# Dilated attention: the biased copy of the input row is made after the split of the projected keys instead of before it

## The chip, the cores and the metric

The kernel runs on one core of one Trainium2 chip. The metric is device time in microseconds (us) for one execution of the whole program; lower is better. The engines named below are TensorE (PE, with its weight loads PEld), VectorE (DVE), ScalarE (ACT), GpSimd (POOL) and SyncE (SP), whose queue issues the transfers between memory and the on-chip buffers.

## The reference, cut to what matters

The program computes six sublayers over x of 16 x 512 x 256, in float32. Only the second one is touched:

```python
x = x + 0.5 * _L0_ffn_ref(_layernorm(x), ...)       # stage f1
x = x + _L0_attn_ref(_layernorm(x), ...)            # stage a1, the changed one
x = x + 0.5 * _L0_ffn_ref(_layernorm(x), ...)       # stage f2
x = x + 0.5 * _L1_ffn_ref(_layernorm(x), ...)       # c1
x = x + _L1_attn_ref(_layernorm(x), ...)            # b1
x = x + 0.5 * _L1_ffn_ref(_layernorm(x), ...)       # c2

# _L0_attn_ref: (branch, offset) pairs (0, 0), (1, 0), (1, 1) with dilations 1, 2, 2
for br, off in pairs:
    xs = x[:, off::r, :].reshape(b_, -1, 128, 256)   # segments of 128 tokens
    att = _mha(xs, Wqkv[br], bqkv[br], Wout[br], bout[br])   # 16 heads of 16
    full = zeros_like(x).at[:, off::r, :].set(att)
res = sum of the three, each times 1/3
```

## The kernel before, in words

The stages run one after another, the attention stage from about 1103 to 2200 us. It handles the 16 batch rows of 512 tokens in turn. A row is eight units of work: four segments of 128 tokens for branch 0 (units u = 0 to 3) and four for branch 1 (u = 4 to 7). A unit t is one segment: PE multiplies queries and keys of 16 heads (`scores`, L1366), DVE takes the maxima (`maximum`, L1566), ACT the exponentials in four groups of heads, here called quads 0 to 3 (`exps`, L1512), PE turns them (`turn_ex`, L1377), DVE copies them (`turned`, L1572), PE multiplies by the values, DVE divides (L1595), and PE and DVE make one eighth of the output of the row before (`put_out`, L1417 and L1604).

Every engine has its own instruction stream, written out by hand in a function `step(t)`; the order within it is the order of execution, and engines meet only at semaphores. Work for later units is done ahead. In unit t, PE projects keys or queries of unit t + 5 (AHEAD is 5), ACT adds the bias and writes the full value and its rounded high part (`project`, L1498; the mark is `a_qk`), and POOL makes the low part: `split_qk(t + AHEAD)`. For queries that is one instruction (L1285). For keys it is five: the difference (L1291), and two copies each of the high and low part, multiplied with the parity of the head (L1296).

POOL has two more jobs in a row r. In unit u = 2 it computes the root and the normalised input of row r + 2 (L135, L137, `scale` L1275), and in unit u = 7 it adds the output bias to the input of row r + 1 (`biased`, L1266: four instructions that read `xt` and write `xb`, mark `g_xb`). Before it does that, `biased(r + 1)` waits until DVE has made the last eighth of the output of row r - 1 (`d_y`), because that output still reads the `xb` buffer of the same parity. POOL reads `xb` for nothing else; DVE uses it one row later.

There are two `xt` buffers. SP's `step(r)` waits for `d_h(r)`, the normalised input made two rows earlier, and for `g_xb(r)`, then issues `load(r + 2)` (L1227, 512 KB), then waits for `d_y(r - 1)` and stores a row (L1243). So the load of row r + 3 waits for `biased(r + 1)`, which is issued in unit u = 7 of row r. DVE needs the loaded row in unit u = 1 of the following row: `half_statistics` (L1632) waits for the load, takes the statistics of two of its four tiles, and takes the other two later in the same unit; the means (L1640) follow in unit u = 2. DVE's order in a unit u = 1 is: divide and turn the next input, maxima of quads 0 and 1, the output part, the reciprocal, the copy of quad 3 of the unit before, the first half of the statistics, the maximum of quad 2, the turned reciprocal, the maximum of quad 3, the copy of quad 0, the second half of the statistics, the copies of quads 1 and 2. PE's `scores(t)` waits for ACT's quad 3 of unit t - 1 and for DVE's copy of quad 2 of unit t - 1, since all share banks of PSUM.

Of the kernel before, what the change touches and what calls it, by code (L numbers as in the profile page):

```python
# [67 lines left out]
def turns(engine, count, unroll, step):  # L68

    groups = count // unroll  # L70
    assert groups * unroll == count and groups >= 2
    for u in range(unroll):
        step(Turn(0, u, unroll))
    if groups > 2:
        with engine.Fori(1, groups - 1) as g:
            for u in range(unroll):
                step(Turn(g, u, unroll))
    for u in range(unroll):
        step(Turn(groups - 1, u, unroll))
# [74 lines left out]
def slot_wait(e, tracks, t):  # L154

    k = len(tracks)
    e.wait_ge(tracks[t.step % k].sem, t.group * (16 * (t.unroll // k)) + 16 * (t.step // k + 1))
# [966 lines left out]
def dilated_attention(nc, name, src, dst, w):  # L1124

    with ExitStack() as ctx:
# [4 lines left out]
        AHEAD = SEGS + 1  # L1131
# [40 lines left out]
        rows, units = B, B * UR  # L1172
# [50 lines left out]
        with nc.Block() as block:  # L1223
            @block.sync
            def _(sp):
                def load(r):
                    sp.dma_start(xt[r.step % 2][:], row_tiles(src, r)).then_inc(s_ld[r.step % 2].sem, 16)  # L1227

                load(first_row)
                sp.dma_start(ident[:], w["ident"]).then_inc(s_id, 16)  # L1230
                for n, (k, t) in enumerate(split):
                    sp.dma_start(raw[n], w[k].rearrange("r (c p) d -> p r c d", p=P)).then_inc(s_raw[n], 16)
                for t, k in ((bq, "abq"), (bk, "abk"), (bv, "abv"), (par, "parity")):
                    sp.dma_start(t[:], w[k]).then_inc(s_p, 16)
                load(first_row + 1)
                sp.dma_start(spread[0:SLOT], w["spread"]).then_inc(s_w, 16)
                sp.dma_start(bo[:].rearrange("p r d -> p (r d)"),
                             w["abo"].rearrange("(o r) d -> o (r d)", o=1).to_broadcast([P, BR * D])).then_inc(s_w, 16)
                sp.dma_start(wo[:], w["ao"].rearrange("r (c p) d -> p r c d", p=P)).then_inc(s_w, 16)

                def store(r):
                    d_y.wait(sp, r)
                    sp.dma_start(row_tiles(dst, r), yt[r.step % 2][:]).then_inc(s_st[r.step % 2].sem, 16)  # L1243

                def step(r):
                    if (r + 2).exists(last=rows):
                        norm.d_h.wait(sp, r)
                        g_xb.wait(sp, r)
                        load(r + 2)
                    if (r - 1).exists():  # L1250
                        store(r - 1)
                turns(sp, rows, ROWS, step)
                store(last_row)
                for k in range(2):
                    sp.wait_ge(s_st[k].sem, 16 * (rows // 2))

            @block.gpsimd
            def _(pool):
                pool.wait_ge(s_c, 1)

                def biased(r):
                    slot_wait(pool, s_ld, r)
                    if (r - 2).exists():
                        d_y.wait(pool, r - 2)
                    for v in range(SEGS):
                        last = pool.tensor_tensor(xb[r.step % 2][:, v, :], xt[r.step % 2][:, v, :], bos[:, 2, :], ALU.add)  # L1266
                    g_xb.mark(last)

                def scale(r):
                    k = r.step % 2  # L1270
                    norm.g_ln.wait(pool, r, "rstd", alone=True)
                    if (r - 1).exists():
                        t_hT.wait(pool, r - 1, "7", alone=True)
                    for v in range(SEGS):
                        last = pool.tensor_scalar(h[:, v, :], xt[k][:, v, :], norm.mv[:, k, v, 0:1],  # L1275
                                                  norm.rstd[:, k, v:v + 1], ALU.subtract, ALU.mult)
                    norm.d_h.mark(last)

                def split_qk(t):
                    br, j = ur_of(t) // SEGS, t.step % SEGS  # L1280
                    c, x = j % DC, full[t.step % 2]
                    a_qk.wait(pool, t)
                    if j >= DC:
                        hi, lo = (a[:, c, :] for a in qT[br])
                        g_qk.mark(pool.tensor_tensor(lo, x[:], hi.bitcast(F32), ALU.subtract))  # L1285
                        return
                    hi = k_hi[t.step % 2]
                    k_mark = Turn(t.group, t.step // SEGS * DC + j, ROWS * UR // 2)
                    if (t - 1).exists():
                        g_qk.wait(pool, t - 1)  # L1290
                    g_kl.mark(pool.tensor_tensor(k_lo[:], x[:], hi[:].bitcast(F32), ALU.subtract))  # L1291
                    for n, part in enumerate((hi, k_lo)):
                        if n:
                            g_kl.wait(pool, k_mark)
                        for e in range(2):
                            last = pool.tensor_tensor(kz[br][n][:, c, e, :], part[:].bitcast(F32),  # L1296
                                                      par[:, e:e + 1].to_broadcast([P, S]), ALU.mult)
                    g_qk.mark(last)

                norm.root(pool, first_row)  # L1300
                norm.root(pool, first_row + 1)
                scale(first_row + 1)
                pool.wait_ge(s_p, 16 * 4)
                for j in range(AHEAD):
                    split_qk(first_unit + j)
                pool.wait_ge(s_b, 4)
                biased(first_row)

                def step(t):
                    u, r = ur_of(t), row_of(t)  # L1310
                    if u == 2 and (r + 2).exists(last=rows):
                        norm.root(pool, r + 2)
                        scale(r + 2)
                    if u == 7 and (r + 1).exists(last=rows):
                        biased(r + 1)
                    if (t + AHEAD).exists(last=units):
                        split_qk(t + AHEAD)
                turns(pool, units, ROWS * UR, step)

            @block.tensor  # L1320
# [1000 lines left out]
```

## Time and profile before

| what | value |
| --- | --- |
| time, median of 3 runs | 4007.72 us (4007.39 to 4008.62) |
| the profiled execution: its time, its span | 4008.62 us, 4006.8 us |
| granted TensorE clock, mean | 0.983 |
| busy over the whole span | PE 95%, PEld 83%, DVE 80%, ACT 77%, POOL 67% |
| mean DMA rate | 35 GB/s |

The profile is one execution. Its span is the time from the first to the last recorded instruction, and 1.8 us of its time lie outside of it. The busy share of PE is modelled and says little by itself: in a stage where engines hand work to one another in a circle, each can look nearly full, while the time is set by the circle. The rows further down are taken from the attention stage.

### The profile page before, as it was taken

What the parts mean: (1) busy time and instruction counts of PE and PEld (TensorE: products, weight loads), DVE (VectorE), ACT (ScalarE), POOL (GpSimd) and SP (SyncE); (2) the same over time, 40 slices, a digit from 0 to 9 for tenths busy, and PEclk for the clock granted to TensorE, in tenths of its full rate; (3) what the DMA queues carried; (4) which work ended last, traced back from release to release, by engine and by line L of the source; (5) the groups of instructions that cost most, each with busy time, mean ns of one, the idle gap of its engine ahead of it and who ended that gap; (6) DMA issues with size and microseconds to landing.
All of it is one profiled execution on the core that took longest, in us unless ns stands there. A gap on an engine that the chain in (4) does not pass through costs nothing. (4 is left out here: it accounts for less than half of the span.)

```text
span 4006.8 us, 81018 instructions
## 1 busy us (share of the span) xinstructions
PE 3796.5 (95%) x28440; PEld 3314.4 (83%) x28440; DVE 3198.6 (80%) x7738; ACT 3098.6 (77%) x7882; POOL 2701.5 (67%) x2202
## 2 busy tenths in 40 slices
PE   7999999999979999999998799999999997999989
PEld 6888888888858888888886688888888887898878
DVE  7888888888758888888875788888888877756667
ACT  6888888888759999999996688888888877632166
POOL 7888888888655554655541788888888866512266
PEclk9999999999989999999999899999999998999999
DMA  2000000000010000000000100000000003331342
GB/s 66 17 17 17 17 17 17 17 17 17 9 44 18 13 23 14 22 23 13 23 7 18 64 17 17 17 17 17 17 17 17 17 12 98 122 105 53 127 151 90
DMA packets 135061, 141.90 MB, mean 35 GB/s; under 512 B 8672, under 2 KB 131968, under 8 KB 134656
## 3 DMA queue, kind: packets, MB, share of 16 engines
q1 hardware_dynamic: 134656, 136.71, 10.7%
q8 instruction: 228, 3.74, 0.4%
q14 instruction: 177, 1.45, 0.1%
HBM read 80.06 MB, written 56.62 MB: 34 GB/s over the span
## 5 line engine op out<-in xcount | busy, mean ns | idle before, releaser
L300 POOL TENSOR_TENSOR f_grid<-f_sim 128x1024 f32<-128x1024 f32 x512 | 969.4, 1910 | 0.1
L1512 ACT ACTIVATE a_ex<-a_p_s,a_mneg 128x128 f32<-128x128 f32 x2048 | 728.2, 409 | 89.9 <-DVE a_mneg L1566 89.9
L686 DVE SCALAR_TENSOR_TENSOR f_p_u<-f_grid,f_te,f_p_dot 128x1024 f32<-128x1024 f32 x512 | 653.2, 1276 | 111.7 <-PE f_p_dot L106 65.3
L308 POOL TENSOR_TENSOR f_q<-f_q 128x1024 f32<-128x1024 f32 x256 | 607.9, 2386 | 123.1 <-ACT f_q L558 121.0
L695 DVE SCALAR_TENSOR_TENSOR f_q<-f_p_u,f_rz,f_grid 128x1024 f32<-128x1024 f32 x512 | 650.9, 1271 | 0.4
L539 ACT ACTIVATE f_grid<-f_grid,f_negm 128x1024 f32<-128x1024 f32 x512 | 559.2, 1142 | 0.0
L1512 ACT ACTIVATION_READ_ACCUMULATOR a_ex<-a_p_s,a_mneg 128x1 f32 x2048 | 508.8, 248 | 0.0
L443 PE MATMUL f_p_y<-f_eup,f_wT 128*128 128x256 f32 x2048 | 472.9, 379 | 0.0
L438 PE MATMUL f_p_y<-f_wdn,f_hs 128*128 128x256 f32 x2048 | 468.4, 382 | 0.0
L443 PEld LDWEIGHTS f_p_y<-f_eup,f_wT 128*128 128x128 f32 x2048 | 388.5, 190 | 57.7
L438 PEld LDWEIGHTS f_p_y<-f_wdn,f_hs 128*128 128x128 f32 x2048 | 378.8, 190 | 49.7
L1566 DVE TENSOR_REDUCE a_mneg<-a_p_s 128x4 f32<-128x512 f32 x512 | 335.0, 675 | 6.7 <-PE a_p_s L1366 6.7
L1572 DVE COPY a_exT<-a_p_s 128x512 f32<-128x512 f32 x384 | 254.4, 684 | 91.9 <-PE a_p_s L1377 91.6
L425 PE MATMUL f_p_wT<-f_ident,f_q 128*128 128x128 f32 x2048 | 269.1, 274 | 22.1 <-POOL f_q L308 20.8
L425 PEld LDWEIGHTS f_p_wT<-f_ident,f_q 128*128 128x128 f32 x2048 | 229.2, 140 | 44.3 <-POOL f_q L308 34.5
L552 ACT ACTIVATE f_hs<-f_p_hid 128x512 f32<-128x512 f32 x256 | 152.1, 594 | 141.4 <-PE f_p_hid L106 140.7
L1377 PE MATMUL a_p_s<-a_ident,a_ex 128*128 128x128 f32 x1536 | 241.6, 283 | 10.6 <-ACT a_ex L1512 10.4
L558 ACT ACTIVATE f_q<-f_q 128x2048 f32<-128x2048 f32 x128 | 244.4, 1909 | 0.0
L287 POOL TENSOR_TENSOR f_cand<-f_tx,f_ty 128x512 f32<-128x512 f32 x128 | 136.9, 1070 | 147.4 <-DVE f_ty L650 147.1
L1377 PEld LDWEIGHTS a_p_s<-a_ident,a_ex 128*128 128x128 f32 x1536 | 166.7, 141 | 53.1 <-ACT a_ex L1512 37.6
L546 ACT COPY f_wT<-f_p_wT 128x512 f32<-128x512 f32 x256 | 148.2, 579 | 76.6 <-PE f_p_wT L425 76.6
L523 ACT COPY f_sim<-f_p_sim 128x512 f32<-128x512 f32 x128 | 74.1, 579 | 142.2 <-PE f_p_sim L106 142.2
(646 smaller groups left out, 11029.3 us busy)
## 6 DMA issues: line engine op xcount, KB each, us to landing
x_f<-f_yt SPq DMA_DIRECT2D x64, 256.0 KB, 2.1
f_xt<-x SPq DMA_DIRECT2D x32, 256.0 KB, 2.9
a_xt<-x_f SPq DMA_DIRECT2D x16, 512.0 KB, 3.8
x_a<-a_yt SPq DMA_DIRECT2D x16, 512.0 KB, 2.9
f_xt<-x_a SPq DMA_DIRECT2D x32, 256.0 KB, 2.9
c_xt<-x_f SPq DMA_DIRECT2D x16, 512.0 KB, 4.7
x_c<-c_yt SPq DMA_DIRECT2D x16, 512.0 KB, 3.1
b1p_xt<-x_c SPq DMA_DIRECT2D x16, 512.0 KB, 3.9
```

The costliest lines, as they stand in the source:

```text
L300: g_grid.mark(pool.tensor_tensor(grid[v][:, hd, :].rearrange("p (i j) -> p i j", i=XROWS), sx[:, hd, :].unsqueeze(2).to_broadcast([P, XROW ...
L308: g_pair.mark(pool.tensor_tensor(q[v][:, 2 * k, :], q[v][:, 2 * k, :], q[v][:, 2 * k + 1, :], ALU.add), f"{v}{k}")
L425: last = pe.matmul(p_wT[:, e, :], q[v][:, hd, (k * HALF + e) * P:(k * HALF + e + 1) * P], ident[:], is_transpose=True, start=hd == 0, stop ...
L438: pe.matmul(p_y[:, v, :], hs[t.step % 2][:, e, v * P:(v + 1) * P], wdn[:, e, :], start=e == 0, stop=False)
L443: last = pe.matmul(p_y[:, v, :], wT[v][:, e, :], eup[:, e, :], start=False, stop=e == EC - 1)
L539: a_exp.mark(act.activation(grid[v][:, hd, :], grid[v][:, hd, :], ACT.Exp, bias=negm[:, v, hd:hd + 1]), f"{v}{hd}")
L686: d_mask.mark(dve.scalar_tensor_tensor(out=p_u[:], in0=grid[v][:, hd, :], scalar=te[:, v, hd, TOP - 1:TOP], in1=p_dot[:], op0=ALU.is_ge, o ...
L695: d_mul.mark(dve.scalar_tensor_tensor(out=q[v][:, hd, :], in0=p_u[:], scalar=rz[:, v, hd:hd + 1], in1=grid[v][:, hd, :], op0=ALU.mult, op1 ...
L1377: last = pe.transpose(p_e[i][:, n, :], ex[t.step % 2][:, i, n, :], ident[:])
L1512: last = act.activation(ex[t.step % 2][:, i, n, :], p_s[i][:, n, :], ACT.Exp, bias=mneg[:, i, n:n + 1], accum_out=z[t.step % 2][:, i, n:n ...
L1566: d_max.mark(dve.tensor_reduce(mneg[:, i, :], p_s[i][:], AX.X, ALU.max, negate=True), str(i))
L1572: d_ex.mark(dve.tensor_copy(exT[t.step % 2][:, i, :, :], p_e[i][:]), str(i))
```

## The change

In POOL's `step(t)` the two last statements change places. In unit u = 7 of each row POOL now does the split of unit t + 5 first, and the biased copy of row r + 1 after it. In the other seven units nothing changes. The other engines' streams and SP's are the same.

```diff
                     if u == 2 and (r + 2).exists(last=rows):
                         norm.root(pool, r + 2)
                         scale(r + 2)
+                    if (t + AHEAD).exists(last=units):
+                        split_qk(t + AHEAD)
                     if u == 7 and (r + 1).exists(last=rows):
                         biased(r + 1)
-                    if (t + AHEAD).exists(last=units):
-                        split_qk(t + AHEAD)
                 turns(pool, units, ROWS * UR, step)
```

In unit u = 7 the split is that of unit t + 5, which is u = 4 of the next row, the first keys of branch 1, so five instructions. POOL's stream around it before, from the last query split of unit 6 to the first instruction of the next unit (`waits` names the semaphores that an instruction waits for; `a_kz1h` and `a_kz1l` are the parity copies of branch 1, `a_k0h` and `a_k1h` the high parts of two successive units):

```order
L1285 TENSOR_TENSOR a_qT0l<-a_full,a_qT0h 128x512 [waits a1_a_qk] x2
L1266 TENSOR_TENSOR a_xb<-a_xt,a_bos 128x256 [waits a1_d_y,a1_s_ld0]
L1266 TENSOR_TENSOR a_xb<-a_xt,a_bos 128x256 x3
L1291 TENSOR_TENSOR a_kl<-a_full,a_k0h 128x512 [waits a1_g_qk,a1_a_qk]
L1296 TENSOR_TENSOR a_kz1h<-a_k0h,a_par 128x512 x2
L1296 TENSOR_TENSOR a_kz1l<-a_kl,a_par 128x512 [waits a1_g_kl]
L1296 TENSOR_TENSOR a_kz1l<-a_kl,a_par 128x512
L1291 TENSOR_TENSOR a_kl<-a_full,a_k1h 128x512 [waits a1_g_qk,a1_a_qk]
```

And the same place of POOL's stream in the changed kernel:

```order
L1285 TENSOR_TENSOR a_qT0l<-a_full,a_qT0h 128x512 [waits a1_a_qk] x2
L1291 TENSOR_TENSOR a_kl<-a_full,a_k0h 128x512 [waits a1_g_qk,a1_a_qk]
L1296 TENSOR_TENSOR a_kz1h<-a_k0h,a_par 128x512 x2
L1296 TENSOR_TENSOR a_kz1l<-a_kl,a_par 128x512 [waits a1_g_kl]
L1296 TENSOR_TENSOR a_kz1l<-a_kl,a_par 128x512
L1266 TENSOR_TENSOR a_xb<-a_xt,a_bos 128x256 [waits a1_d_y,a1_s_ld0]
L1266 TENSOR_TENSOR a_xb<-a_xt,a_bos 128x256 x3
L1291 TENSOR_TENSOR a_kl<-a_full,a_k1h 128x512 [waits a1_g_qk,a1_a_qk]
```

The four instructions of L1266 have moved behind the five of one key split, with their waits for the output and the load; this happens once in each of 15 rows, and no instruction is added or removed.

## Rows read from the trace of the kernel before

**Rows 1.** Stretch, us, busy PE PEld DVE ACT POOL, granted clock, DMA: units u=1, 2:

```profile
1606.90:1614.92 8.02, 8.02 (x99) 6.77 (x98) 7.60 (x18) 7.41 (x38) 7.88 (x8) 1.00 0.09 31
1614.92:1622.94 8.02, 8.02 (x99) 6.77 (x98) 6.67 (x18) 7.40 (x38) 3.24 (x5) 1.00 0.01 2
```

**Rows 2.** Timeline (start us, us, engine, line), first scores of two units:

```profile
1606.92 0.39 PE L1366 MATMUL a_p_s<-a_kz0l,a_qT0h 32*128 32x256 f32 x4
...
1614.94 0.39 PE L1366 MATMUL a_p_s<-a_kz0l,a_qT0h 32*128 32x256 f32 x4
```

**Rows 3.** Timeline, ACT, from unit u = 7 to u = 1:

```profile
1599.27 0.81 ACT L1498 ACTIVATE a_k0h<-a_p_pr,a_bk 128x512 fp32r<-128x512 f32 x1
...
1606.36 0.31 ACT L1512 ACTIVATION_READ_ACCUMULATOR a_ex<-a_p_s,a_mneg 128x1 f32 x1
...
1608.72 0.37 ACT L1512 ACTIVATE a_ex<-a_p_s,a_mneg 128x128 f32<-128x128 f32 x1 [0.61 <-DVE a_mneg L1566]
...
1611.73 0.42 ACT L1512 ACTIVATE a_ex<-a_p_s,a_mneg 128x128 f32<-128x128 f32 x1
```

**Rows 4.** Timeline, SP queue, same stretch:

```profile
1601.42 0.36 SPq L1243 DMA_DIRECT2D x_a<-a_yt  x1
1604.40 0.36 SPq L1227 DMA_DIRECT2D a_xt<-x_f  x1
```

**Rows 5.** Timeline, POOL, same stretch:

```profile
1601.53 2.79 POOL L1266 TENSOR_TENSOR a_xb<-a_xt,a_bos 128x256 f32<-128x256 f32 x4 [8.11 <-DVE a_yt L1604]
1604.28 1.27 POOL L1291 TENSOR_TENSOR a_kl<-a_full,a_k0h 128x512 fp32r<-128x512 f32 x1
...
1607.51 2.03 POOL L1296 TENSOR_TENSOR a_kz1l<-a_kl,a_par 128x512 fp32r<-128x512 f32 x2
```

**Rows 6.** All issues of L1227, the loads of a_xt:

```profile
L1227 SPq DMA_DIRECT2D a_xt<-x_f x16: 359/360/525, 1106.2 to 1989.6; - x16
...
DMA to landing us min/median/max: 3.7/3.8/6.2
```

**Rows 7.** Timeline, DVE, unit u = 1 and start of u = 2:

```profile
1610.04 0.73 DVE L1632 BATCH_NORM_STATS2 a_bs<-a_xt 128x6 f32<-128x256 f32 x2
1610.69 0.67 DVE L1566 TENSOR_REDUCE a_mneg<-a_p_s 128x4 f32<-128x512 f32 x1
...
1613.43 1.31 DVE L1572 COPY a_exT<-a_p_s 128x512 f32<-128x512 f32 x2
...
1615.97 1.28 DVE L1566 TENSOR_REDUCE a_mneg<-a_p_s 128x4 f32<-128x512 f32 x2
```

**Rows 8.** Timeline, POOL, start of the stage and end of row 0:

```profile
1145.19 1.27 POOL L1291 TENSOR_TENSOR a_kl<-a_full,a_k0h 128x512 fp32r<-128x512 f32 x1 [3.01 <-ACT a_k0h L1498]
...
1150.47 2.77 POOL L1266 TENSOR_TENSOR a_xb<-a_xt,a_bos 128x256 f32<-128x256 f32 x4
...
1183.07 1.29 POOL L1291 TENSOR_TENSOR a_kl<-a_full,a_k0h 128x512 fp32r<-128x512 f32 x1 [3.78 <-ACT a_k0h L1498]
...
1191.06 1.28 POOL L1291 TENSOR_TENSOR a_kl<-a_full,a_k1h 128x512 fp32r<-128x512 f32 x1 [2.70 <-ACT a_k1h L1498]
...
1214.99 1.29 POOL L1291 TENSOR_TENSOR a_kl<-a_full,a_k0h 128x512 fp32r<-128x512 f32 x1 [3.93 <-ACT a_k0h L1498]
```

**Rows 9.** Timeline, SP queue, start of the stage, two issues merged:

```profile
1153.32 58.18 SPq L1227 DMA_DIRECT2D a_xt<-x_f  x2
```

**Rows 10.** Timeline, DVE, statistics of row 3:

```profile
1224.84 0.73 DVE L1632 BATCH_NORM_STATS2 a_bs<-a_xt 128x6 f32<-128x256 f32 x2
```

**Rows 11.** Source L1296, who waited for it (us, times):

```profile
  ACT a_full L1498: 9.3, 2
```

**Rows 12.** Busy time and granted clock, start of the stage, 2 us each:

```profile
1151.00:1153.00 2.00, 1.11 (x8) 0.64 (x7) 0.80 (x2) 2.00 (x14) 2.00 (x4) 1.00 0.00 0
1153.00:1155.00 2.00, 1.12 (x5) 0.93 (x5) 0.59 (x1) 2.00 (x14) 0.24 (x1) 0.65 0.15 27
1155.00:1157.00 2.00, 1.34 (x21) 1.16 (x24) 1.18 (x3) 1.38 (x4) 0.54 (x1) 0.50 0.74 244
```

## The prediction

> **What bounds the kernel now.** I read the busy table first, but it does not decide. In the attention stage a unit takes 8.02 us: PE's first scores of two successive units start at 1606.92 and 1614.94 [rows 2]. PE is shown busy for all 8.02 us of both units, ACT for 7.4, DVE for 7.60 in the unit with the statistics (u = 1) and 6.67 in the next [rows 1]. PE is not what sets the 8.02. In row 0 PE has no output part to make, and POOL's splits still follow one another after 7.99 us, 1183.07 to 1191.06 [rows 8].
>
> So I looked for a circle in the timelines. ACT's last exponential of a unit ends at 1606.36 + 0.31 = 1606.67; PE starts the next scores at 1606.92; DVE takes their maxima, and ACT's first exponential starts at 1608.72, after 0.61 us of waiting for DVE's maximum [rows 2, 3]. From 1606.67 to 1608.72 are 2.05 us, and the rest of the 8.02, 5.97 us, is ACT's 16 exponentials and a copy, back to back. The circle has no slack, neither in u = 1 nor in the other units, whose starts are 8.02 us apart as well. Whatever holds it once is lost for good.
>
> Now the load. SP issues the load of `xt` at 1604.40, 0.08 us after POOL's biased copy ended at 1601.53 + 2.79 = 1604.32 [rows 4, 5]. A load lands after 3.8 us (median of 16; the 6.2 is one at the start among the weights) [rows 6], so at 1608.20. DVE starts its statistics of it at 1610.04, without waiting [rows 7]. The slack is 1.84 us. All of the forecast comes from that slack.
>
> **What the change gives.** The key split in u = 7 no longer waits for the biased copy. The high part of the keys is ready at 1599.27 + 0.81 = 1600.08 [rows 3], the split started at 1604.28 [rows 5]; it will start at 1600.16, 4.12 us sooner. Nobody gains: its keys are read by the scores of unit t + 5, which also need three more splits of the row, and the only waits for the product of a key split are two, 9.3 us together [rows 11], in front of ACT's projections at the start of the stage, ahead of the first u = 7. POOL was idle 8.11 us before the copy [rows 5]; an idle POOL is worth nothing. This term is 0.
>
> **What it moves back.** The copy now stands behind five instructions. The same order, a five-instruction key split, then the copy, then a load, exists once in the trace before: at the start of the stage POOL starts a split at 1145.19 and the copy at 1150.47 [rows 8], and SP issues the load at 1153.32 [rows 9]. From split start to issue 8.13 us. The other way to work it out agrees: split 1604.28 to 1607.51 + 2.03 = 1609.54, or 5.26, plus 2.79 for the copy and 0.08, makes 8.13 [rows 4, 5]. The copy's other wait, for the output, is over by 1601.53 [rows 5], and no longer counts.
> - Load issued: 1600.16 + 8.13 = 1608.29, which is 3.89 later than before.
> - Landed: + 3.8 = 1612.09.
> - DVE wanted it at 1610.04: 2.05 us of waiting, in u = 1 of the next row.
>
> The store of the row before goes out at 1601.42 in either kernel [rows 4] and stands ahead of this load in SP's queue; the store behind it waits for an output made 60 us later. So SP is no term.
>
> **What is queued behind the wait.** DVE runs in order. Behind the statistics stand the maxima of quads 2 and 3, on which ACT's second half rests, and the copies of quads 0, 1 and 2. The maximum of quad 2 ended at 1610.69 + 0.67 = 1611.36, ACT's first exponential of quad 2 began at 1611.73 [rows 3, 7]: 0.37 us of slack. ACT's path is thus 2.05 - 0.37 = 1.68 late. DVE's path is worse: from 1610.04 until its last copy ends at 1613.43 + 1.31 = 1614.74 it is full [rows 7], and PE's next scores, which wait for that copy, start at 1614.94 [rows 2]. They start the full 2.05 late, and the maxima behind them, at 1615.97 [rows 7], as well. I take 2.05 a row. The bounds are 1.68 (only ACT's path counts) and 2.25 (PE adds, to a wait that is now real, the 0.20 us between 1614.74 and 1614.94 once more).
>
> **How often.** The trace has 16 loads [rows 6]. Two are issued ahead of the loop and one behind the copy of row 0, none of them changed. The other 13 stand behind a copy in u = 7. The first is no exception, though its copy does not wait for an output: it was issued at 1153.32 + 58.18 - 0.36 = 1211.14 [rows 9]; now it is 1214.99 + 8.13 = 1223.12 [rows 8], landed at 1226.92, wanted at 1224.84 [rows 10], 2.08 late. The copies of the last two rows gate no load, and their output is a row away: 0. After a held unit all engines are late by the same amount and the next row starts with the same distances, so the waits add.
>
> **Sum.** 13 x 2.05 = 26.7 us. The profiled execution took 4008.62 us (span 4006.8 and 1.8 around it), giving 4035.3; from the median of the runs, 4007.72, which I use, it is 4034.4. The bounds: 13 x 1.68 = 21.8, or 4029.6, and 13 x 2.25 = 29.3, or 4037.0. The landing time could differ, since the load no longer follows a store: 3.7 is the shortest seen [rows 6], 1.3 us less in the sum; each further 0.1 us on it costs 1.3 more.
>
> The landing row says 3.8 us for 512 KB [rows 6]. The Trainium skill (DMA: Bandwidth & Descriptors, "Anatomy of one DMA — SWDGE (gpsimd) path") puts a transfer at about 2.0 us fixed plus its bytes over 436 GB/s, fitted on transfers that GpSimd issues. By that page a load would land after 3.2 us, an estimate; the wait would be 1.45 us, the sum 18.9 and the time 4026.6. The trace does not agree with it here, and its 3.8 is used.
>
> **Rivals.**
> - *The cover holds: not slower.* The place is DVE in u = 2 to 7. There it is busy for 6.67 of 8.02 us [rows 1], so it could catch up 1.35 us in a unit, and ACT idles 0.61 us in each [rows 3]. If these idle times were room, the 2.05 us would be gone after two to four units, and the time would be 4007.7. It decides if a held unit is followed by units shorter than 8.02. Against it: the idle times are waits inside the circle, and the unit of row 0, with less work on PE, is no shorter than 7.99 [rows 8]. To stay within 8 us of the time before, only 0.62 of the 2.05 us may be left. 4 in 100.
> - *Part of it is made up.* With PE shown full, but by modelled ends, and ACT's path 1.68 late, something like 1.0 to 1.5 us a row may stay: 13 to 20 us, 4021 to 4027. It needs DVE's last copy to have had slack ahead of the scores, for which only the 0.20 us speak. 9 in 100.
> - *The clock falls as well.* While DVE waits, PE waits for turned exponentials. At the start of the stage PE was busy for 1.11 and 1.12 us in two stretches of 2 us, and the granted clock went from 1.00 to 0.65 and then 0.50, the 1.2 GHz level [rows 12]. In a held u = 1 unit PE would do 8 us of work in 10, and in the 4 us around the gap clearly less. If each gap brought on some 4 us at the low level, up to 2 us of PE's work more a row would be exposed: 13 x 4.05 = 52.7, or 4060. Against it: there the thin work went on for a third stretch, with 1.34 us of 2 [rows 12], while here a full unit follows at once; and in row 0, where PE had idle time in each unit, splits kept coming every 7.99 us [rows 8]. 7 in 100. The Trainium skill (TensorE: Matmul & The Clock Gate, "HAM oscillation — how this bites in real kernels") has a kernel whose loop falls to the low clock again after the wait for a load in each pass. That the level falls after gaps in PE's work, the rows at the start of the stage agree with.
> - *Faster.* It would need someone who waits for the key split of u = 7. No row shows one. 1 in 100.
> - *The forecast*, 4029 to 4038: 79 in 100.
>
> **How the numbers follow.** Less than 0.2% (8 us) of change can't be told from none here. Slower by more: 79 + 9 + 7 = 95 in 100. Within it: 4. Faster: 1. The range of 8 in 10 takes the forecast's bounds and the landing time's, and reaches into the part-recovered case below and towards the clock's above: 4026 to 4041.
>
> **What would show it.** In the changed profile:
> 1. SP's issues of L1227 come about 3.9 us later against DVE's statistics in their row; rows are 8 x 8.02 + 2.05 = 66.2 us apart instead of 64.2.
> 2. DVE has 13 waits for the DMA of `a_xt` at L1632, of 2.0 to 2.1 us, 27 us together; before, it had none.
> 3. POOL starts the key split right behind ACT's high part, and its idle time in front of the copy is gone.
> 4. ACT's wait for the maxima grows by 13 x 1.7 to 2.05 us, and the units u = 2 to 7 still take 8.02.
> 5. The granted clock stays at 1.00 in the stage.
>
> It is wrong if DVE doesn't wait for the load (the issue is not late, or it lands sooner), if the units after a held one are shorter than 8.02, or if the time is outside 4026 to 4041.

## The result

The changed kernel took 4046.96 us (median of 4 runs, 4038.94 to 4051.94), the kernel before beside it 4007.55 us (4 runs, 4005.32 to 4008.62). The ratio is 1.0097, with a 95% interval of 1.0080 to 1.0115. It is slower, as forecast, but by 39.4 us where 26.7 were forecast, and the time lies outside the range of 4026 to 4041. The profiled execution took 4039.2 us (span 4037.1), 8 us less than the median and inside the range. The four runs of the changed kernel differ by 13 us and those of the kernel before by 3 us; that need not be a property of the two kernels, since the changed one differed by 3.6 us in a second set of runs (after_again) and the one before by 10 us in a set of 23.

### The profile page after: what moved, and what is told of

The parts are those of the page before. It is cut to its first block and busy times, and to the rows that moved or that the text cites. A ratio compares the mean times of both kernels' runs of the same rounds, so it can differ in the third digit from the quotient of the medians.

```text
span 4037.1 us, 81018 instructions
## 1 busy us (share of the span) xinstructions
PE 3804.1 (94%) x28440; PEld 3320.2 (82%) x28440; DVE 3198.6 (79%) x7738; ACT 3100.6 (77%) x7882; POOL 2701.7 (67%) x2202
## 3 DMA queue, kind: packets, MB, share of 16 engines
q14 instruction: 177, 1.45, 0.1%
## 5 line engine op out<-in xcount | busy, mean ns | idle before, releaser
L1377 PE MATMUL a_p_s<-a_ident,a_ex 128*128 128x128 f32 x1536 | 241.3, 283 | 10.9 <-ACT a_ex L1512 9.9
```

Of the source, the lines that this page charges most:

```text
L1377: last = pe.transpose(p_e[i][:, n, :], ex[t.step % 2][:, i, n, :], ident[:])
```

## The profile after

First the chain that was forecast, in one row of the stage. POOL and the SP queue around a unit u = 7, columns as before: start, duration, engine and line, operation, and in brackets the idle time ahead with what ended it.

```profile
1677.62 1.30 POOL L1291 TENSOR_TENSOR a_kl<-a_full,a_k0h 128x512 fp32r<-128x512 f32 x1 [6.73 <-ACT a_k0h L1498]
1678.88 2.04 POOL L1296 TENSOR_TENSOR a_kz1h<-a_k0h,a_par 128x512 fp32r<-128x512 f32 x2
1680.88 2.04 POOL L1296 TENSOR_TENSOR a_kz1l<-a_kl,a_par 128x512 fp32r<-128x512 f32 x2
1682.88 2.81 POOL L1266 TENSOR_TENSOR a_xb<-a_xt,a_bos 128x256 f32<-128x256 f32 x4
```

```profile
1545.43 0.36 SPq L1243 DMA_DIRECT2D x_a<-a_yt  x1
1552.30 0.36 SPq L1227 DMA_DIRECT2D a_xt<-x_f  x1
1612.81 0.36 SPq L1243 DMA_DIRECT2D x_a<-a_yt  x1
1619.66 0.36 SPq L1227 DMA_DIRECT2D a_xt<-x_f  x1
1678.89 0.36 SPq L1243 DMA_DIRECT2D x_a<-a_yt  x1
1685.76 0.36 SPq L1227 DMA_DIRECT2D a_xt<-x_f  x1
1746.30 0.36 SPq L1243 DMA_DIRECT2D x_a<-a_yt  x1
```

From the split's start (1677.62) to the load's issue (1685.76) are 8.14 us; 8.13 were taken from [rows 8, 9]. The load is issued 6.87 us after the store of the row, where before it was 2.98 [rows 4]: 3.89 us later, as worked out. POOL now starts the split behind ACT's high part, and no idle time stands in front of the copy, as forecast. But look at the stores: 1545.43 to 1612.81 are 67.38 us, the next row 66.08, the next 67.41. The forecast had 66.2 for all.

What the late load does to DVE, ACT and PE, in the same row:

```profile
1689.50 0.75 DVE L1632 BATCH_NORM_STATS2 a_bs<-a_xt 128x6 f32<-128x256 f32 x2 [1.90 <-DMA a_xt<-x_f]
...
1690.88 0.37 ACT L1512 ACTIVATE a_ex<-a_p_s,a_mneg 128x128 f32<-128x128 f32 x1 [1.52 <-DVE a_mneg L1566]
...
1691.08 0.71 PE L1410 MATMUL a_p_vr<-a_rzT,a_spread 32*128 32x128 f32 x4 [1.44 <-DVE a_rzT L1584]
```

DVE's statistics wait 1.90 us where they waited for nothing [rows 7]. ACT waits for the maximum behind them. PE, though, does not wait for ACT but for the small turned table of reciprocals (L1584), which stands behind the same statistics in DVE's order; it feeds `repeat`, and PE has nothing else to do meanwhile. In the kernel before, PE ran into the same product without a wait:

```profile
1612.10 0.71 PE L1410 MATMUL a_p_vr<-a_rzT,a_spread 32*128 32x128 f32 x4
```

The stage's waits in sum (us, times, longest), one line for DVE and one for PE:

```profile
DVE a_bs L1632 <- DMA a_xt<-x_f: 27.8, 14, 2.2
...
PE a_p_vr L1410 <- DVE a_rzT L1584: 19.9, 13, 1.7
```

Of the 14 waits 13 belong to the held rows, 25.8 us together; the fourteenth, 1.98 us, is at the start of the stage behind a load that took 5.2 us. The 13 waits are of two sizes by turns, about 1.9 and 2.1 us, because the loads land by turns after 3.7 and 3.8 to 4.0 us, in the kernel before as well. Where the clock stays up, the units after a held one still take 8.02 us.

The second part is in the granted clock. Windows of 2 us of one of the longer rows (stretch, its length, busy time of PE, PEld, DVE, ACT and POOL, clock, DMA share, GB/s):

```profile
1553.00:1555.00 2.00, 2.00 (x15) 1.71 (x13) 1.14 (x4) 2.00 (x13) 2.00 (x3) 1.00 0.64 202
1555.00:1557.00 2.00, 1.18 (x34) 0.81 (x32) 0.95 (x3) 0.91 (x5) 2.00 (x3) 1.00 0.22 73
1557.00:1559.00 2.00, 1.31 (x9) 0.95 (x9) 2.00 (x5) 1.57 (x9) 0.48 (x1) 1.00 0.00 0
1559.00:1561.00 2.00, 2.00 (x11) 2.00 (x12) 1.62 (x4) 2.00 (x10) 0.00 (x0) 0.60 0.00 0
1561.00:1563.00 2.00, 2.00 (x28) 1.68 (x26) 0.92 (x3) 0.76 (x2) 1.16 (x1) 0.55 0.00 0
1563.00:1565.00 2.00, 2.00 (x15) 1.70 (x12) 1.86 (x5) 1.07 (x7) 0.12 (x1) 1.00 0.00 0
```

PE's gap lies in the second and third stretch; then the clock is at its low level (1.2 GHz) for about 3.4 us and back at 1.00. PE does its usual work in that time, at half the clock:

```profile
1557.63 0.71 PE L1410 MATMUL a_p_vr<-a_rzT,a_spread 32*128 32x128 f32 x4 [1.45 <-DVE a_rzT L1584]
1558.27 1.50 PE L1377 MATMUL a_p_s<-a_ident,a_ex 128*128 128x128 f32 x8
1559.56 0.42 PE L1328 MATMUL a_p_ox<-a_ident,a_h 128*128 128x128 f32 x1
1559.77 1.91 PE L1417 MATMUL a_p_ox<-a_wo,a_oT 128*128 128x128 f32 x8
1561.61 0.58 PE L1366 MATMUL a_p_s<-a_kz0l,a_qT0h 32*128 32x256 f32 x4
```

The same eight products of L1417 take 1.06 us in the row after, where the clock stays up:

```profile
1625.11 0.71 PE L1410 MATMUL a_p_vr<-a_rzT,a_spread 32*128 32x128 f32 x4 [1.56 <-DVE a_rzT L1584]
1625.75 1.37 PE L1377 MATMUL a_p_s<-a_ident,a_ex 128*128 128x128 f32 x8
1626.96 0.27 PE L1328 MATMUL a_p_ox<-a_ident,a_h 128*128 128x128 f32 x1
1627.07 1.06 PE L1417 MATMUL a_p_ox<-a_wo,a_oT 128*128 128x128 f32 x8
1628.25 0.39 PE L1366 MATMUL a_p_s<-a_kz0l,a_qT0h 32*128 32x256 f32 x4
```

The gap in front is no shorter there (1.56 against 1.45 us). A first held row stands ahead of the first store of the stage; its clock stayed up, behind a gap of 1.73 us. Of the twelve rows between the first and the thirteenth store, seven are long (67.2 to 67.6 us) and five short (65.9 to 66.2). All rows before were 64.2 us. The clock was low for 23.9 us in these rows, and never before.

## Experiments

The theory: a held row costs DVE's wait, less a little, and in some rows the gap that it makes in PE's work brings the clock down, which costs again. The rival for the second part: the executions and rows differ in how long the load takes to land. The rival for the first: the early key split costs or gives something by itself.

The number to compare is the sum of the twelve row lengths (store to store, SP queue), which leaves out what the other stages do, and also the start and the end of this one, the first held row among them. What lies outside the twelve rows was 3236.5 us in the profile before, 3235 to 3243 in the profiles of the changed kernel with and without filling, and between 3232 and 3248 in all, so a single time of this program can be some 10 us away from what its twelve rows say. Each ratio is to the kernel before, run beside it. The rows come from one profiled execution of each kernel. "Low" is the time at the low clock within the twelve rows, from windows of 2 us.

| kernel | median, us | ratio (95%) | 12 rows over before, us | long rows | low, us |
| --- | --- | --- | --- | --- | --- |
| before | 4007.6 to 4011.0 | 1 | 0 (770.33) | 0 | 0 |
| changed | 4046.96 | 1.0097 (1.0080 to 1.0115) | 31.6 | 7 | 23.9 |
| after_again | 4044.62 | 1.0087 (1.0073 to 1.0101) | 33.9 | 8 | 27.3 |
| pe_fed | 4038.38 | 1.0071 (1.0058 to 1.0083) | 22.9 | 0 | 0 |
| pe_fed_5 | 4038.32 | 1.0073 (1.0060 to 1.0087) | 22.5 | 0 | 0 |
| late_stats | 4016.77 | 1.0016 (1.0007 to 1.0025) | 4.2 | 0 | 0 |
| before_late_stats | 4011.08 | 1.0008 (0.9999 to 1.0017) | 4.2 | 0 | 0 |
| before_fed | 4024.84 | 1.0036 (1.0024 to 1.0049) | 13.7 | 0 | 0 |
| dose_3 | 4015.90 | 1.0013 (1.0004 to 1.0022) | 4.9 | 1 | 3.4 |
| dose_4 | 4023.69 | 1.0033 (1.0022 to 1.0044) | 12.3 | 0 | 0 |
| dose_6 | 4053.66 | 1.0111 (1.0097 to 1.0125) | 42.2 | 10 | 34.1 |
| dose_6_fed | 4047.54 | 1.0095 (1.0081 to 1.0108) | 29.0 | 0 | 0 |

**after_again: the changed kernel once more.** No edit.

> The changed kernel once more, to see what differs between its executions. Theory (wait and clock): each of 13 rows is held by DVE's wait for its load, about 1.86 us, which alone gives 4007.5 + 24.2 = 4032; in some or all of them the granted clock then falls for some 3.5 us, 1.35 us more a row. 8 of 13 rows would give 4042.5, all 13 rows 4049. So the runs lie between 4032 and 4050, spread over more than 5 us, and the profile has rows of two lengths, about 66.0 and 67.4 us. Rival (landing): the executions differ in how long the load takes; then the waits at the statistics in the profile differ by a microsecond or more from row to row, and the clock has no part in it.

Measured: 4044.62 us (4043.78 to 4047.37); eight rows of 67.3 to 68.2 us and four of 65.9 to 66.1. The two lengths are there, and not the rival's picture: in the first profile the long rows had waits of 1.86 to 2.12 us and the short ones of 1.87 to 2.17. One row in this profile, of 68.2 us, has a late load (it landed after 4.5 us, a wait of 2.71). The time range was right, but the spread of 3.6 us in this set is less than the 5 expected.

**late_stats and before_late_stats: the need for the load moved instead of the load.** In the changed kernel and in the one before:

```diff
-                    if u == 1 and (r + 2).exists(last=rows):
-                        half_statistics(r + 2, 0)
...
                     if u == 1 and (r + 2).exists(last=rows):
+                        half_statistics(r + 2, 0)
                         half_statistics(r + 2, 1)
```

> The changed kernel with both halves of the statistics at the second of their two places in unit u = 1, 2.6 us later in DVE's stream. If the whole loss comes through the load's slack, DVE wants the row at about 1612.68 minus 0.73 of removed work, 1611.95, on the time scale of before, and the load lands at 1612.09: a wait of about 0.1 us is left, the clock stays up, and the time is 4007 to 4011. If the early start of the key split costs something by itself, or the late copy holds anything else, it stays above 4020. A second risk, the same in both theories: 0.65 us of statistics more between the maximum of quad 3 and the copies of quads 1 and 2 may hold the unit by up to 0.7 us a row, 9 us in all, since DVE's slack there was 0.76 us.

> The kernel before with both halves of the statistics at the second place. The load has landed long before (1608.20 against about 1611.95), so no DMA wait in any theory. It shows what the later place costs by itself: nothing, 4007.5, if DVE's 0.76 us gap ahead of the copies of quads 1 and 2 takes the 0.65 us; up to 0.7 us a row, 4016, if it doesn't. A gain is possible only if the earlier maximum of quad 2 were of use to ACT, which has 0.37 us of slack there: none expected.

Measured: 4016.77 and 4011.08 us. In both profiles every row has the same length, 64.54 us, no DVE wait for a load at the statistics, and no low clock. So in the rows the two orders of POOL's work are the same to 0.01 us once the load has slack: the early split gives and costs nothing, and the whole loss comes through the load. The later place costs 0.35 us a row by itself, half of the 0.7 that was the bound. The late_stats median missed the expected 4007 to 4011; about 4.6 us of it is the price of the later place in 13 rows. The two medians differ by 5.7 us although the rows don't. The kernel before differs as well between the two sets, and by the ratios 3.2 us are left. Both ratios allow the 4.6 us within their intervals, and the two intervals overlap. Where the difference comes from isn't known: the profile of late_stats is its fastest execution (4008.76 of up to 4021.37), and the slower ones, of a slightly lower mean clock, left no trace. So the rows show no cost of the early split, and the times leave room for a few us.

Two stores in a row of each kernel, late_stats first:

```profile
1602.35 0.36 SPq L1243 DMA_DIRECT2D x_a<-a_yt  x1
1666.88 0.36 SPq L1243 DMA_DIRECT2D x_a<-a_yt  x1
```

```profile
1601.60 0.36 SPq L1243 DMA_DIRECT2D x_a<-a_yt  x1
1666.13 0.36 SPq L1243 DMA_DIRECT2D x_a<-a_yt  x1
```

**pe_fed and pe_fed_5: PE kept at work in the gap.** In the changed kernel, with ten and with five products:

```diff
                         attend(t - 1)
+                        if u == 1 and (r + 2).exists(last=rows) and (r - 1).exists():
+                            for _ in range(10):
+                                pe.transpose(p_h, ident[:], ident[:])
                         repeat(t - 1)
```

> The changed kernel with ten extra PE transposes of a constant per row, in unit u = 1, between the product with the values and the one that spreads the reciprocals, just where PE stands still for about 1.6 us while DVE waits for the load. They use idle time only. Wait and clock: the waits stay (13 of about 2.1 us), the clock stays at 1.00 in the attention stage, and the time falls from the changed kernel's 4047 to 4031 to 4036 and spreads less. Rival (landing, or a longer wait in the slow executions): the extra products change nothing, 4047, or add up to 1 us a row, 4060.

> The changed kernel with five instead of ten extra transposes a row in the gap, so 0.6 us of 1.5 filled. Wait and clock: if that is enough, rows of 66.1 us throughout, no low clock, 4038 as with ten. If not, some rows of 67.3 us remain, fewer than the 7 or 8 of 12 without them, and the time is between 4038 and 4045.

Measured: 4038.38 and 4038.32 us, the first 6.2 us under the changed kernel in the same set. The runs of the two kernels don't overlap (4036.71 to 4041.16 against 4043.78 to 4047.37). The waits are still there (the ten-product kernel's line of waits), and the clock is not low in any row:

```profile
DVE a_bs L1635 <- DMA a_xt<-x_f: 26.4, 13, 2.7
```

The windows of the same stretch of its stage, and PE's timeline in it; L1467 is the filling:

```profile
1555.00:1557.00 2.00, 2.00 (x33) 1.75 (x35) 0.48 (x1) 2.00 (x13) 2.00 (x3) 1.00 0.72 247
1557.00:1559.00 2.00, 1.85 (x31) 1.42 (x23) 1.68 (x5) 0.55 (x3) 1.83 (x2) 1.00 0.00 0
1559.00:1561.00 2.00, 1.94 (x15) 1.58 (x16) 2.00 (x5) 2.00 (x13) 0.00 (x0) 1.00 0.00 0
1561.00:1563.00 2.00, 1.88 (x34) 1.59 (x32) 1.81 (x5) 2.00 (x7) 0.00 (x0) 1.00 0.00 0
```

```profile
1557.45 1.31 PE L1467 MATMUL a_p_ox<-a_ident 128*128 128x128 f32 x10
1558.91 0.71 PE L1410 MATMUL a_p_vr<-a_rzT,a_spread 32*128 32x128 f32 x4
1559.54 1.37 PE L1377 MATMUL a_p_s<-a_ident,a_ex 128*128 128x128 f32 x8
1560.75 0.27 PE L1328 MATMUL a_p_ox<-a_ident,a_h 128*128 128x128 f32 x1
1560.86 1.06 PE L1417 MATMUL a_p_ox<-a_wo,a_oT 128*128 128x128 f32 x8
```

The rows are 65.9 to 66.2 us, with one of 66.8 behind a wait of 2.75, and add 22.9 us over twelve rows: 1.91 each. More work on PE made the kernel faster. The difference to the changed kernel's rows is 31.6 - 22.9 = 8.7 us, and 33.9 - 22.9 = 11.0 for the second execution. The waits of the three differ a little, pe_fed's one of 2.75 above all. If each row is instead given its own wait less 0.12 us (the price of a wait with the clock up, from the doses below), the first execution of the changed kernel has 9.4 us left for 23.9 us at the low clock, and the second 10.9 for 27.3: 0.39 and 0.40 us lost for each us at the low level. With five products a gap of 0.69 to 0.99 us was left on PE in each row, and the clock stayed up all the same. Both kernels are a little above the range of 4031 to 4036 for ten products; it was counted from 4007.5, and the kernel before took 4011.0 beside pe_fed.

**before_fed: the same filling where there is no gap.** The edit of pe_fed in the kernel before.

> The kernel before with the same ten transposes a row at the same place, where PE has no gap to put them in. They are about 1.2 us of PE work. If PE is full in a unit, as its busy time says, each of 13 rows gets 1.2 us longer: 4023. If the circle of exponentials, scores and maxima sets the unit and PE only looks full, much of it is taken up in the 0.8 us that the output part leaves in row 0: 4007 to 4014.

Measured: 4024.84 us, each row 65.33 us: 1.14 us a row for ten products that took 1.31 us in the gap. The first of the two expectations held. At this place of PE's order there is next to no room.

**dose_3, dose_4, dose_6: the old order, a later load.** In the kernel before, k tiles of the biased copy are written again (with a mark of its own for each pass, whose lines are left out here):

```diff
-                    for v in range(SEGS):
+                    for n in range(SEGS + k):
+                        v = n % SEGS
+                        if n and v == 0:
+                            g_xb.wait(pool, r, str(n // SEGS))
                         last = pool.tensor_tensor(xb[...], xt[...], bos[:, 2, :], ALU.add)
```

> The kernel before, its order kept, with three of the four tiles of the biased copy written a second time before the copy is marked done (from row 1 of the loop on, and in the copies ahead of it). The load is issued about 2.2 us later; the slack is 1.84. Wait about 0.4 us a row, the clock stays up: 4007.5 + 13 x 0.4 = 4012, range 4009 to 4016. If it is not the load but the order of the split that costs, 4007.5.

> As the dose of three, with all four tiles written twice: the load about 2.9 us later, a wait of about 1.1 us a row, 14 us in all: 4021 if the clock stays up, up to 4038 if it falls in every row. If a wait below 1 us were absorbed by the following units, 4007.5.

> As the dose of three, with six tiles written again: the load about 4.4 us later, a wait of about 2.6 us a row. Wait and clock: 13 x (2.4 + 1.35) = 49, about 4056, with the clock falling in nearly every row and so little spread; without the clock 4039. That the early split and not the load costs the time would give 4007.5.

Measured: 4015.90, 4023.69 and 4053.66 us. The key split stays behind the copy, and the time rises with the lateness of the load. The first of the 13 loads still landed in time, so 12 rows are held and not the 13 of the expectations. Two waits of dose_3 in two successive rows:

```profile
1351.92 0.75 DVE L1636 BATCH_NORM_STATS2 a_bs<-a_xt 128x6 f32<-128x256 f32 x2 [0.34 <-DMA a_xt<-x_f]
...
1417.83 0.75 DVE L1636 BATCH_NORM_STATS2 a_bs<-a_xt 128x6 f32<-128x256 f32 x2 [1.84 <-DMA a_xt<-x_f]
```

and two of dose_4:

```profile
1355.50 0.75 DVE L1636 BATCH_NORM_STATS2 a_bs<-a_xt 128x6 f32<-128x256 f32 x2 [1.04 <-DMA a_xt<-x_f]
...
1421.27 0.75 DVE L1636 BATCH_NORM_STATS2 a_bs<-a_xt 128x6 f32<-128x256 f32 x2 [1.71 <-DMA a_xt<-x_f]
```

Their rows were 64.42, 67.16, 65.10 and 65.77 us. Over the 64.19 of before these are 0.23, 2.97, 0.91 and 1.58. Where the clock stays up a row is longer than the same row of before by the wait less 0.10 to 0.14 us, at every dose, and pe_fed's waits of 1.85, 2.07 and 2.75 with rows 1.72, 1.97 and 2.63 longer lie on the same line. One row of dose_3 had a load that landed after 5.4 us instead of 3.8; why isn't known. Its clock fell, and it cost 1.25 us more than the line. dose_4, with waits up to 1.71 us, had no fall in these rows; in dose_6, with some 2.5 us, ten of twelve rows had one.

The gaps in front of L1410 put the runs in one order. No gap of 0.35 to 1.25 us was followed by a fall (12 in dose_4, 12 in pe_fed_5, 6 in pe_fed, one in dose_6_fed). Of 37 gaps of 1.36 to 2.67 us (12 rows each of the changed kernel's two executions and of dose_6, and the one row of dose_3) 26 were. The shortest before a fall was 1.39 us, the longest without one 2.12 us.

**dose_6_fed: the filling at the largest dose.** The filling of pe_fed, 18 products, in dose_6.

> The kernel before with six tiles of the biased copy written again (the load some 4.4 us later, a wait of 2.7 us a row) and 18 extra PE transposes of a constant in PE's gap in unit u = 1. Without them that kernel took 4053.7, its rows 3.52 us over 64.19, with 34 us at the low clock in twelve rows. Wait and clock: the clock stays up, the rows fall to 64.19 + 2.6 = 66.8 and the time to 4010 + 13 x 2.6 = 4044 (4041 to 4047). If the low clock were a companion of the longer rows and not a cause, 4054 or more.

Measured: 4047.54 us, rows 66.4 to 67.1, 29.0 us over twelve rows where dose_6 had 42.2, no low clock, and the DMA waits unchanged (30.4 us in twelve, in both). 13.2 us for 34.1 us at the low level is 0.39 us each, as above. The rows are where they were expected. The medians show less: against the kernel before the ratio falls only from 1.0111 to 1.0095, 6 us, with intervals that overlap. The profiled execution lost part of the gain outside the twelve rows, which was 3248 us where dose_6 had 3240; why isn't known.

## Why the prediction was wrong

- *The key split earlier: 0.* Right. 64.54 us a row with either order, once the load has slack.
- *The load issued 3.89 us later, DVE 2.05 us waiting, 13 times.* Right: 3.89 us, waits of 1.86 to 2.19 us, 25.8 us in the 13 rows against 26.7. That it paid nothing back in the following units was right too: they took 8.02 us with the clock up, and even dose_4's waits of about 1 us were paid but for 0.12, which leaves nothing of the rivals in which the wait is covered or partly made up. The long split in front of the copy was read from the start of the stage to 0.01 us.
- *What is queued behind the wait.* The full 2.05 us was taken; a held row costs the wait less 0.12 us, so the 13 rows cost 25.84 - 13 x 0.12 = 24.3 us, and 24.9 in the second execution. The bound of 1.68 by ACT's path alone was too low. PE was named as waiting for the copy of quad 2; the wait that shows is for the turned reciprocals of L1584, which also stand behind the statistics and which the prediction left out. That wait makes the gap in PE's work.
- *The clock.* This is the step that failed: the sum has no term for the granted clock, and its fifth sign was that the clock stays at 1.00 in the stage. The prediction had the fall as a rival of 7 in 100, at up to 2 us a row in every row, and let none of it into the forecast. It happened in seven and in eight of 13 held rows, at 1.2 to 1.5 us each, and filling the gap on PE took it away. The argument against it was that a full unit follows the gap at once, and that row 0 has idle time on PE without a fall. Neither helps: a gap of 1.45 us in an otherwise full unit was enough, in some rows and not in others, and the thin work of [rows 12] was nearer to this case than the steady rows, which have no such gap.
- *PE is not what sets the 8.02 us.* Half right. The output part of PE is free in row 0, and the unit is no shorter there; but ten products ahead of `repeat` cost 87% of their time in before_fed. So a delay of PE at that place is paid almost in full. Which part of PE's order is full besides wasn't tested.
- *The sum.* 4034.4 was forecast from waits alone, and the kernels with the clock kept up took 4038.4 and 4038.3, with ratios of 1.0071 and 1.0073 where the forecast is 1.0067. With the ratio of pe_fed the first set would have been at 4036, inside the range, so the waits alone don't miss it. The clock adds 9.4 and 10.9 us, all in the twelve rows, as the first held row had no fall. Waits and clock give 33.7 and 35.9 us; the medians say 39.4 and 33.6.
- *Left open.* The median of the first set, 4046.96, is 8 us above the profiled execution, and some 6 us of the 39.4 are in neither waits nor clock as the profile has them. Its three slower runs show mean granted clocks of 0.977 to 0.978 where the two at 4039 show 0.980, so more time at the low level; in which rows or stages isn't known, as they have no trace. Nor was it found what decides, among gaps of 1.36 us and more, in which rows the clock falls; the length of the gap does not.

No version beat the kernel before. Its load has 1.84 us of slack, and nothing here showed a use for more.

## What to carry to other kernels

When two statements of one engine change places, follow the marks of the one that is now later to the transfers that they release, and set the new lateness against the slack at the reader; the statement that is now earlier is worth only what somebody waited for it. If the reader stands in the closed chain of a steady loop, count the wait in full for each pass, and then look at what TensorE does in that time: a new gap of a microsecond and a half in a full stage can cost the clock on top of the wait, and a handful of products on a constant in that gap shows whether it does, and takes that part back.

## What the runs showed of the hardware

- In this stage a gap of 1.4 to 1.7 us on PE, with full work around it, was followed by about 3.4 us at the low clock in 7 of 12 rows; in a second execution, with gaps of 1.36 to 1.66 us and one of 2.25, in 8 of 12. With 5 or 10 small products in it (0.77 or 1.31 us) it was so in none of 24, and gaps of 0.43 to 1.25 us (dose_4) had no fall either.
- A microsecond at the low level cost 0.39 to 0.40 us of time here, less than half. That PE waits for others in part of it may be why; it wasn't tested.
- The load of 512 KB landed in 3.6 to 4.0 us, by turns nearer 3.7 and 3.9, whether it was issued 3.0 or 6.9 us behind the store; single loads took 4.3 to 5.4 us, in the kernel before as well (its last, 4.3). In the profile of the kernel before a slack of 1.84 us covered all 13.
